# A graph block with a mixture of experts on one core: tokens sent to tiles of their two experts, 20 dense sets for 12, 8 gathered tiles per unit

## The reference, cut to what matters

```python
# x (6250, 256), 200000 edges (src, dst), sorted by dst
xn = layernorm(x)
# GNN: mean of the neighbours' rows
neigh = segment_sum(xn[src], dst, 6250) / max(degree, 1)
g = relu(concat(xn, neigh) @ gnn_W + gnn_b);  g = g / norm(g)
# linear attention over all nodes, 8 heads of 32
q, k, v = split(xn @ Wqkv);  q = softmax(q, in the head) * 32**-0.5;  k = softmax(k, over the nodes)
mixed = layernorm((q @ (k.T @ v per head)) @ Wout) * gamma
x = x + g + mixed
# experts: each token uses 2 of 8
t = layernorm(x);  logits = t @ router_w.T
weights = the two largest of softmax(logits), scaled to sum 1
out = t
for e in range(8):
    out = out + weight of e for this token * (gelu(t @ w1[e] + b1[e]) @ w2[e] + b2[e])
return x + out
```

## Time and profile before

| | |
|---|---|
| Median of 3 runs | 1843.57 us (1842.81 to 1844.68) |
| Profiled execution: span from first to last instruction | 2433.1 us |
| Busy of the span | PE 76%, PEld 60%, POOL 53%, DVE 50%, ACT 28% |
| Mean granted TensorE clock | 0.908 |
| Instructions | 34393 |
| Setup; B1; B2; head; main stage | 66; 364; 260; 35; 1708 us of the span |

### The profile page before, as it was taken

The page is one execution under the profiler, slowest core; times in us unless marked ns, Lnnn a source line. Parts: engine busy times, 40 slices in busy tenths (PEclk is TensorE's granted clock), DMA queues, the critical chain, the costliest instruction groups (busy, mean ns, idle before and its releaser), DMA issues.

```text
span 2433.1 us, 34393 instructions
## 1 busy us (share of the span) xinstructions
PE 1851.1 (76%) x11044; PEld 1449.7 (60%) x11044; DVE 1222.2 (50%) x4533; ACT 685.0 (28%) x1736; POOL 1277.6 (53%) x1310
## 2 busy tenths in 40 slices
PE   0578877878748787787887787877778777777888
PEld 0355555666526665666666666666666666666677
DVE  8322222442235555455555555555555555555576
ACT  6333333332202222222222222222222222222233
POOL 1655565464655654655555555655555555545510
PEclk9899999998868988988989998988998989988999
DMA  7445554443642332322332332332332322322310
GB/s 256 140 147 158 161 158 142 121 118 106 183 120 79 98 94 66 100 77 85 98 89 80 90 94 83 94 89 76 91 92 84 90 85 85 90 81 84 92 42 13
DMA packets 144715, 251.14 MB, mean 103 GB/s; under 512 B 28046, under 2 KB 96062, under 8 KB 144542
## 3 DMA queue, kind: packets, MB, share of 16 engines
q0 software_dynamic: 62352, 170.35, 24.6%
q1 hardware_dynamic: 82190, 78.59, 10.1%
HBM read 216.74 MB, written 32.09 MB: 102 GB/s over the span
## 4 chain that ended last, share of the span: by engine, by line
PE 47%; another core or an unknown queue 22%; DVE 11%; issue 11%; ACT 8%; DMA 1%; SPq 1%; POOL 0%; DVEq 0%; POOLq 0%; ACTq 0%
PE ps_hidden L867 9%; PE ps_expert L878 9%; PE ps_zone L653 3%; PE ps_zone L655 3%; PE ps_proj L832 3%; PE ps_proj L805 2%; PE ps_proj L835 2%; ACT sb_stage L1039 2%; PE ps_zone L697 2%; PE ps_turned L662 2%; PE ps_zone L699 2%; PE ps_hidden L761 2%; PE ps_proj L761 2%; PE ps_expert L687 1%
## 5 line engine op out<-in xcount | busy, mean ns | idle before, releaser
L609 POOL DMA_INDIRECT sb_ring<-xn_table,sb_idx x1299 | 1270.1, 978 | 1050.4 <-PE ps_zone L655 485.3
L878 PE MATMUL ps_expert<-sb_arena,sb_stage 128*128 128x256 f32 x1568 | 444.7, 408 | 61.4 <-DVE sb_arena L1531 34.0
L1039 ACT ACTIVATE sb_stage<-ps_hidden,sb_b_col 128x128 f32<-128x128 f32 x784 | 241.7, 365 | 874.3 <-remote 469.1
L867 PE MATMUL ps_hidden<-sb_arena 128*128 128x128 f32 x3136 | 458.5, 293 | 27.7 <-ACT sb_stage L1039 21.0
L867 PEld LDWEIGHTS ps_hidden<-sb_arena 128*128 128x128 f32 x3136 | 415.8, 206 | 64.6 <-issue 30.7
L1531 DVE SCALAR_TENSOR_TENSOR sb_arena<-ps_expert,sb_small,sb_arena 128x256 f32<-128x256 f32 x392 | 189.0, 482 | 337.1 <-remote 211.6
L653 PE MATMUL ps_zone<-sb_ring,sb_onehot 128*128 128x256 f16 x1299 | 336.6, 287 | 22.6 <-issue 12.4
L878 PEld LDWEIGHTS ps_expert<-sb_arena,sb_stage 128*128 128x128 f32 x1568 | 287.4, 204 | 99.5 <-issue 58.3
L655 PE MATMUL ps_zone<-sb_ring,sb_onehot 128*128 128x257 f16 x1299 | 337.1, 288 | 6.2 <-issue 6.2
L655 PEld LDWEIGHTS ps_zone<-sb_ring,sb_onehot 128*128 128x128 f16 x1299 | 133.5, 103 | 62.6 <-issue 19.3
L653 PEld LDWEIGHTS ps_zone<-sb_ring,sb_onehot 128*128 128x128 f16 x1299 | 134.6, 104 | 51.5 <-issue 14.5
(11 more groups left out here) (175 smaller groups left out, 2267.8 us busy)
## 6 DMA issues: line engine op xcount, KB each, us to landing
sb_ring<-xn_table,sb_idx POOLq DMA_INDIRECT x1299
keys_values<-sb_stage SPq DMA_DIRECT2D x49, 256.0 KB
sb_stage<-keys_values SPq DMA_DIRECT2D x96, 128.0 KB
sb_sums<-x SPq DMA_DIRECT2D x7, 896.0 KB, 11.1
sb_stage<-x SPq DMA_DIRECT2D x49, 128.0 KB
xn_transposed<-sb_stage SPq DMA_DIRECT2D x49, 128.0 KB
sb_arena<-xn_transposed SPq DMA_DIRECT2D x49, 128.0 KB
sb_arena<-x SPq DMA_DIRECT2D x49, 128.0 KB
```

The source lines that it names most:

```text
L609: pool.indirect_dma_start(ring3[:, place, 0:2 * D], None, table, bass.IndirectOffsetOnAxis(tile_idx, 0)).then_inc(signal, 16)
L867: mm = pe.matmul(hidden[e % 2][:, j * P:(j + 1) * P], w1_sb[:, e, c, j * P:(j + 1) * P], halves(tokens_t[b % 2])[:, c, :], start=c == 0, s ...
L878: mm = pe.matmul(expert[e % 2][:, 0:D], halves(act_h[e % len(act_h)])[:, c, :], w2_sb[:, e, c, :], start=c == 0, stop=c == KC - 1, skip_gr ...
L1039: ins = act.activation(halves(act_h[e % len(act_h)])[:, j, :], hidden[e % 2][:, j * P:(j + 1) * P], ACT.Gelu, bias=b1_col[:, e * KC + j:e ...
```

## The change

The experts no longer run for all tokens of a block. DVE keeps each token's two choices and weights (`picks`, `routes`), and the blocks are taken in five cohorts of 13, 12, 11, 8 and 5 blocks. When the last block of a cohort is routed, PE counts the tokens per expert (`rank`), DVE turns counts into row numbers (`dispatch`, 15 links of a chain), and POOL scatters the tokens, one indirect DMA per block and choice, to DRAM tiles of 128 rows that belong to one expert each. A cohort of n blocks has 2n+7 such tiles; there are 133 in all. A tile is a job: SP reads its expert's number (a TENSOR_LOAD), loads the packed weights (128 x 1026 fp32) and the 128 tokens; PE transposes them (`turn_sent`), ACT copies, `up`, Gelu, `down`, ACT copies the answer (`copy_answer`), SP stores it. A tick does the transposes of job n, `up` of n-1 and `down` of n-2. When all jobs of a cohort are stored, POOL fetches each block's two rows per token with two more indirect DMAs (`fetch_answers`), and DVE adds them with their weights to the stored base rows (`finish`). Scatters and fetches are 98 each. The main stage has 392 steps as before and 34 more behind them for the last cohorts' jobs and blocks; 19 ticks and 15 of the 49 `finish` lie behind step 392. In pass B1 SP also clears the 133 tiles (17 MB of zeros), and before it packs the weights in DRAM (4 MB).

Of the 1563 edge tiles 440 are now in 20 dense sets and 1123 are gathered: 784 in the passes (8 per unit), 16 in the head, 323 in the main stage (0.86 per step).

```diff
-SETS = 12
+SETS = 20
...
-B1_TILES, B2_TILES = 4, 3
-B1_DENSE, B2_DENSE = 2.1, 2.7
+B1_TILES, B2_TILES = 8, 8
+B1_DENSE, B2_DENSE = 2.7, 4.8
...
-MAIN_RATE = 2.6
-EARLY_EXPERTS = 6
+SLOTS = 8
+MAIN_RATE = 0.86
+POOL_LEAD = 16
...
+W_BUFS, T_BUFS = 5, 4
+TOKEN_RING = 19
+
+COHORTS = (13, 12, 11, 8, 5)
...
+            def load_job(n):
...
+                e = sp.value_load(owner[0:1, n:n + 1], min_val=0, max_val=EXPERTS - 1)
+                wait(sp, expert_filled, n - W_BUFS + 1)
+                sp.dma_start(w_bufs[n % W_BUFS], pack[bass.ds(e * P, P), :]).then_inc(w_landed[n % W_BUFS], 16)
+                wait(sp, sent_turned, n - T_BUFS + 1)
+                row = (n - JOB_FIRST[g]) * P
+                sp.dma_start(sent_in[n % T_BUFS], sent[g][row:row + P, :]).then_inc(sent_landed[n % T_BUFS], 16)
...
+            ahead = MAIN_TILE + POOL_LEAD
+            gather_tiles(range(ahead))
+            for m, e, tiles, scatters, ticks, stores, loads_now, finals in STEPS:
+                until = min(GATHER_TILES, tiles.stop + POOL_LEAD)
+                gather_tiles(range(ahead, until))
+                ahead = until
+                for b, choice in scatters:
+                    scatter(b, choice)
+                for b in loads_now:
+                    fetch_answers(b)
...
+            def tick(n):
+                if n < JOBS:
+                    turn_sent(n)
+                if 1 <= n <= JOBS:
+                    up(n - 1)
+                if n >= 2:
+                    down(n - 2)
...
-                up(m, e)
-                if m * EXPERTS + e >= LAG:
-                    down(m * EXPERTS + e - LAG)
+                for n in ticks:
+                    tick(n)
...
+                chain.link(dve.tensor_tensor(picked16[:, mine], pick1, pick2, ALU.add))
+                chain.link(dve.tensor_tensor(so_far16[:, after], so_far16[:, mine], picked16[:, mine], ALU.add))
...
-            def add_expert(n):
-
-                b, e = divmod(n, EXPERTS)
-                dve.wait_ge(expert_filled, n + len(act_h) + 1)
-                wait(dve, expert_added, n)
-                dve.scalar_tensor_tensor(out=out_sb[b % 2], in0=expert[e % 2][:, 0:D],
-                                         scalar=combine[b % 2][:, e:e + 1], in1=out_sb[b % 2],
-                                         op0=ALU.mult, op1=ALU.add).then_inc(expert_added, 1)
...
+            def finish(b):
+
+                dve.wait_ge(base_landed[b % 2], b // 2 * 16 + 16)
+                dve.wait_ge(y_landed[b % 2], b // 2 * 32 + 32)
+                for choice in (0, 1):
+                    dve.scalar_tensor_tensor(out=base_in[b % 2], in0=y_rows[b % 2][choice],
+                                             scalar=routes[:, 2 * b + choice:2 * b + choice + 1], in1=base_in[b % 2],
+                                             op0=ALU.mult, op1=ALU.add).then_inc((finish_chain, block_done)[choice], 1)
```

More of the change, by code:

```diff
@@ L328, in by_head @@
             return ap.rearrange("p (h c) -> p h c", h=HEADS)
[L331 to L338, removed]
+        xnt = [buf(arena, n) for n in (0, 1)]
@@ L341, in gps_kernel @@
+        owner_sum = arena[0:1, 29 * D + 16:29 * D + 16 + max(JOBS_OF)]
+        owner = arena[0:1, 29 * D + 64:29 * D + 64 + JOBS].bitcast(I32)
+        tokens = [buf(arena, 30 + n) for n in range(TOKEN_RING)]
+        assert (30 + TOKEN_RING) * D <= BLOCKS * (2 * D + 2) // 2
         xn_b = buf(stage, 0)
@@ L574, in _ @@
+            for b in late:
+                store_out(b)
             for n in (0, 1):
@@ L903, in _ @@
             project(1)
-            for m, e, tiles in STEPS:
-                nxt, after = m + 1 < BLOCKS, m + 2 < BLOCKS
+            for m, e, tiles, scatters, ticks, *_ in STEPS:
+                nxt, after = m is not None and m + 1 < BLOCKS, m is not None and m + 2 < BLOCKS
                 sum_tiles(tiles)
@@ L925, in _ @@
                         turn_tokens(m + 1)
-            for n in range(BLOCKS * EXPERTS - LAG, BLOCKS * EXPERTS):
-                down(n)
         @block.scalar
@@ L1055, in _ @@
                     act.activation(combine_t, turned[0:EXPERTS, 0:P], ACT.Copy).then_inc(turn_read, 1)
-                gelu(m, e)
+                for n in ticks:
+                    tick(n)
                 if e == 0:
@@ L1602, in _ @@
                         start_output(m + 1, heads[m])
+                if e == 2 and m in LAST_OF:
+                    dispatch(COHORT[m])
                 for _ in meanwhile:
                     pass
-                if m * EXPERTS + e >= LAG:
-                    add_expert(m * EXPERTS + e - LAG)
-                if e == EXPERTS - 1 and after:
+                for b in finals:
+                    finish(b)
+                if e == SLOTS - 1 and after:
                     split_projection(m + 2)
                 add_zones(tiles)
-            for n in range(BLOCKS * EXPERTS - LAG, BLOCKS * EXPERTS):
-                add_expert(n)
 def constants():
```

394 lines of the change are left out of this document (321 added, 73 removed).

## The result

The changed kernel takes **2420.94 us** (median of 4 runs, 2416.68 to 2425.0) against 1843.19 us before (4 runs, 1839.93 to 1844.68): a ratio of 1.3147, 95% interval 1.312 to 1.3173. Slower, as forecast, but by 578 us where 377 were forecast, and outside the range that ended at 2330.

What follows compares the result with a forecast made beforehand. It took POOL's gathers to bound the kernel before, PE and DVE close behind; afterwards gathers bound the passes, DVE's chain the blocks. 66 + 1004 + 20 + 966 + 78 + 60 + 25 = 2219, 2220 us; range 1890 to 2330.

Steps and rivals of the forecast that it cites:

- What bounds the kernel before: Whole kernel before: without the profiler's pauses POOL's gathers stand almost end to end; PE and DVE within a few per cent.
- A gather takes 1.25 us of the queue: POOL's queue: a gather of 0.95 us plus 0.30 us not counted before the next; 1.26 main stage, 1.33 passes.
- Rival 1: Passes: gathers take say 0.9 us outside the profiler, so PE sets the pace; total 1927 us; chance 0.20.
- The passes, 1004 us: Passes B1 and B2: POOL's 784 gathers at 1.28 us each are the bound, while PE needs 7 us a unit.
- the ring lets POOL go 24 tiles, 30 us, ahead, so I cost it at nothing: Start of B1: the weight pack before the first load is covered by POOL running ahead; cost nothing.
- not that every batch costs its whole length: Passes: DVE's wide comparisons lock POOL's port only partly; taken whole, 110 batches x 1.28 would add 141 us.
- The main stage, 21.0 us a block: Main stage: DVE's chain sets the block, from 22.8 us before to 21.0, for 46 blocks 966 us.
- the low clock and its price: Main stage, part of the slower rival: less PE work lowers its clock, chain about 2.4 us longer, block 24 us.
- The end, 78 + 60 + 25: Last three blocks at 26 us, 19 ticks behind step 392 at 3.2, then five blocks of fetches, `finish` and store.
- SP's TENSOR_LOAD per job stands one tick ahead of its use and is hidden until a tick is shorter than the load: End, behind the last steps: the per-job load on SP's queue is covered; a tick taken as 3.2 us.
- Scatter and fetch at a gather's price: POOL in the main stage: no row showed a scatter; costed at 1.25 us, bounds nothing and 1.97.
- Rival 3: Slower still: PE's low clock in the main stage and the DVE port lock in the passes, 2300 to 2400; chance 0.09.

Runs made afterwards that it cites:

- the shorter chain: DVE's square roots with one Newton step for three, made to both kernels: changed kernel 2328.6 us, kernel before 1834.2 us.

## Why the prediction was right in its direction and short in its size

**What bounds the kernel before: right.** Pauses of one profile, gathers end to end without them, PE a few per cent behind: all three are shown by the second profile.

**A gather takes 1.25 us of the queue: right, and it decides.** In the changed kernel's passes the first 24 tiles go out at that pace, then the ring is full:

```profile
98.38 0.94 POOL L765 DMA_INDIRECT sb_ring<-xn_table,sb_idx  x1 [0.30 <-issue]
99.62 0.94 POOL L765 DMA_INDIRECT sb_ring<-xn_table,sb_idx  x1 [0.30 <-issue]
117.51 0.94 POOL L765 DMA_INDIRECT sb_ring<-xn_table,sb_idx  x1 [16.94 <-PE ps_zone L848]
```

PE waits for the tiles in its place: in the passes 242.9 us before weight loads and 164.6 before products. Rival 1 (a gather shorter outside the profiler) is out: this profile is of an execution of 2423.6 us, and the others took 2416.7 to 2425.0.

**The passes, 1004 us: 58 too low.** By the forecast the first `split_projection` starts near 66 + 1004 + 3 = 1073; it starts at 1130.8. (Three more kernels with the same passes start it at 1123 to 1128, so some 8 of the 58 may be chance.) Of these 58, 30 are the gather's price: 1018 + 300 = 1318 ns and not 1280, x 784. Another 18 are POOL's waits for PE, nearly all of them the one above. This is the step "the ring lets POOL go 24 tiles, 30 us, ahead, so I cost it at nothing": PE stood still longer than 30 us, because ACT waited 42.1 us for the first block of `x`:

```profile
ACT sb_stage L1208 <- DMA sb_stage<-x: 42.1, 1, 42.1
```

That load is behind the pack of the weights in SP's queue: SP issues the pack from 61.7 us on and comes to the first load of `x` at 96.7. (That the pack is what holds it is read from these times; no run moved it. The kernel before with 8 tiles, without a pack, waits 3.4 us in all.) The last 10 are a later first gather (70.0 us for 66.9), three gathers more and the landing of the last.

**The port, "not that every batch costs its whole length": right.** It costs 0.4 to 0.5 us for a comparison of 1.28. By the rule of the Trainium skill (SBUF — State Buffer, "SBUF: two separate sides") taken whole, 44 comparisons fewer should have given 56 us; with 12 sets "up to" was 14 to 22 us shorter.

**The main stage, 21.0 us a block: 1.9 too low.** Cut at the same two points, the forecast has 20 for the head, 46 x 21.0 and one block of 26, 1012 us; the 48 intervals took 1104, 92 more. That DVE's chain bounds the blocks is shown by the shorter chain, with a gain in the changed kernel alone. Two steps failed.

First, I named the low clock and its price, and put it among the rivals and not into the sum. It came in the first 16 blocks: 0.64, the wait for `mix` 2.06 us longer than in the earlier trace rows, where I had given 2.4. Keeping PE busy takes 1.9 us off each of these blocks, 29 us in all. The sentence by the Trainium skill (TensorE: Matmul & The Clock Gate, "HAM oscillation — how this bites in real kernels") gave the right mechanism; the block that I had worked out for it was 24 us, and the interval there was 22.0. These 16 intervals took 354 us for the 335 of the forecast, and 325 with PE kept busy, so the rest of the chain was costed 10 us too high there, which hid a part of the clock's price.

Second, and more, 73 of the 92 us lie in the 32 later intervals (23.4 us), where I gave the ticks no effect on the chain. There 1.1 us an interval, 36 us, is the tokens' late arrival, as the run with loads two ticks ahead shows. The other 37 stay open. The longest intervals are 38.2 us (the last, at whose end DVE waits 8.5 us for `project`), 30.5, 29.8 and 28.0. Only that of 30.5 holds a cohort's `dispatch`, which takes 4.3 us there; the other three intervals with one take 23 to 26. The clock is 0.81 to 0.86 in these blocks, and no run raised it there.

**The end, 78 + 60 + 25: 50 too low.** The forecast has 137 us behind the last `split_projection` (two blocks of 26, 60 and 25); it was 187. The failed step is "SP's TENSOR_LOAD per job stands one tick ahead of its use and is hidden until a tick is shorter than the load". I set 3.2 us for a tick by the bytes, and loads issued one tick ahead, whose cost I had put at nothing, made it 4.8. What PE waits for is not the TENSOR_LOAD but the transfer of the tokens behind it: 54.4 us in 26 waits. 19 ticks x 1.6 are 30, and the 16 before them, at 5.0 us for 3.25, 27 more; what follows the last tick was a little shorter than forecast. Loads ahead give back 31.

The three add up: 58 + 92 + 50 = 200, against 2421.7 - 2219 = 203; the 3 missing are those from the passes' end to the first `split_projection`, which the forecast counts within the head.

**Scatter and fetch at a gather's price: right.** They measure 999 and 955 ns:

```profile
L812 POOL DMA_INDIRECT sb_arena<-answers,sb_arena x98 | 93.6, 955 | 261.0 <-DVE sb_arena L1827 158.5
...
L798 POOL DMA_INDIRECT sent_tokens<-sb_arena x98 | 97.9, 999 | 70.9 <-DVE sb_arena L1805 42.3
```

**The range.** Rival 3 is the one that came nearest (2300 to 2400), and I gave it 0.09. The clock and the dearer gather stood in that rival, priced but held unlikely, and the late loads stood nowhere; all three push one way. The range should have gone as far above the forecast as their sum.

## What to carry to other kernels

Count what passes through the engine that is the bound. The change took 690 us of expert work from PE, by the prediction's rows, and gave it the jobs, eight more sets and a lower clock instead (busy 1635 us for 1656 in all); and it took not one indirect DMA from POOL: 1299 before, 1123 + 98 + 98 = 1319 after. What then decides is where they stand. Before, they are spread as PE's work is, and both engines are full; after, 784 stand where PE has too little to do, and the other 535 where POOL waits for DVE's chain.

A load issued one step ahead is covered only while the step is longer than the load's time to land; compare the two before costing it by its bytes. And work taken from TensorE can make the products that are left slower: in a chain that waits for one of them, the clock belongs into the sum.

## What was unexpected of the hardware

One profile of a kernel held 590 us of pauses, with "remote" as the releaser of 152.5 us of POOL's waits, and a second profile of it had none; the span beside the median of the runs told it. And 80 added matrix products per block, of no use, made a kernel 29 us faster, by a clock of 0.96 for 0.64.
